# First batch of a fused attention and feed-forward kernel: the query down projection in two token halves, masks made in a room of their own, raw weights of heads 3 and 4 ahead of two stores

## The reference

```python
kv_c = kv @ W_kvc                     # 1024 -> 256
q_c = layernorm(x) @ W_dq             # 1024 -> 384
q_nope, q_rope = q_c @ W_uq, rope(q_c @ W_qr)
k_nope, v, k_rope = kv_c @ W_uk, kv_c @ W_uv, rope(kv_c @ W_kr)
scores = (q_nope . k_nope + q_rope . k_rope) / sqrt(192)
scores = where((k_ids <= seg) & (k_ids >= seg - 8), scores, -1e30)
x = x + (softmax(scores) @ v) @ W_o
```

## Time and profile before

| what | us |
|---|---|
| median of 3 runs (lowest, highest) | 3100.45 (3096.45, 3101.98) |
| the profiled execution, its own time | 3100.04 |
| its span | 3098.2 |
| PE busy | 3002.1 (97%) |
| DVE busy | 2109.3 (68%) |
| ACT busy | 1524.8 (49%) |
| POOL busy | 708.2 (23%) |

### The profile page before, as it was taken

How to read it: one execution, slowest core, us unless ns; L and a number is a source line. 1 busy time by engine, 2 the same in 40 slices (tenths; PEclk the granted TensorE clock), 3 DMA queues, 4 the chain that set the end, 5 groups by cost and what they waited for, 6 DMA issues and landing times.

```text
span 3098.2 us, 40880 instructions
## 1 busy us (share of the span) xinstructions
PE 3002.1 (97%) x14242; PEld 2432.5 (79%) x14242; DVE 2109.3 (68%) x4519; ACT 1524.8 (49%) x2983; POOL 708.2 (23%) x533
## 2 busy tenths in 40 slices
PE   7999999999999999999999999999999999999985
PEld 4788878888888878888788888888888887888862
DVE  3555657777577766777667775777757776677776
ACT  2655525555355544555345453555535554455553
POOL 6223141110411114111321114111041111411127
PEclk9999999999999999999999999999999999999985
DMA  6654456443644446344554445644364444544431
GB/s 220 228 177 165 163 212 201 146 143 117 230 157 142 142 174 218 129 144 141 183 190 144 147 137 190 208 143 136 116 237 157 146 142 174 195 135 142 146 92 4
DMA packets 163242, 496.48 MB, mean 160 GB/s; under 512 B 36689, under 2 KB 50641, under 8 KB 138337
## 3 DMA queue, kind: packets, MB, share of 16 engines
q1 hardware_dynamic: 157968, 493.00, 47.6%
q0 software_dynamic: 5072, 0.88, 0.7%
HBM read 387.68 MB, written 72.55 MB: 149 GB/s over the span
## 4 chain that ended last, share of the span: by engine, by line
PE 87%; DVE 5%; POOL 2%; DMA 2%; issue 1%; ACT 1%; SPq 0%; DVEq 0%; POOLq 0%; ACTq 0%
PE psD L2187 10%; PE psC L2196 10%; PE psE L2196 10%; PE psA L2118 8%; PE psT L2174 6%; PE psB L2127 5%; PE psA L2078 4%; PE psS L2155 4%; PE psD L2138 4%; PE psS L2161 4%; PE psS L2157 3%; PE psS L2156 3%; PE psS L2158 3%; PE psB L2078 2%; PE psA L2109 2%; PE psB L2109 2%
## 5 line engine op out<-in xcount | busy, mean ns | idle before, releaser
L1176 ACT ACTIVATE exps_ring<-exps_ring,neg_max 128x512 f32<-128x512 f32 x512 | 370.8, 724 | 421.9 <-DVE neg_max L1535 421.2
L1535 DVE CUSTOM_DVE_ANT_0 exps_ring<-psS,mask 128x512 f32<-128x512 f32 x512 | 353.1, 690 | 290.7 <-PE psS L2161 287.8
L1190 ACT ACTIVATE probsT_hi<-psT 128x512 fp32r<-128x512 f32 x472 | 282.4, 598 | 339.1 <-PE psT L2174 337.2
L1182 ACT ACTIVATE exps_ring<-exps_ring,row_sum_inverse 128x512 f32<-128x512 f32 x512 | 369.7, 722 | 60.8 <-DVE row_sum_inverse L1541 60.8
L1547 DVE TENSOR_TENSOR probsT_lo<-psT,probsT_hi 128x512 fp32r<-128x512 f32 x472 | 323.8, 686 | 55.0 <-ACT probsT_hi L1190 53.3
L2196 PE MATMUL psC<-w_o_pair,attn_hi 128*128 128x512 f32 x1016 | 333.8, 409 | 0.7 <-DVE attn_lo L1553 0.7
L2196 PE MATMUL psE<-w_o_pair,attn_hi 128*128 128x512 f32 x896 | 295.3, 410 | 0.0
L2174 PE MATMUL psT<-ident,exps_ring 128*128 128x128 f32 x1888 | 283.2, 272 | 5.6 <-DVE probsT_lo L1547 4.6
L2174 PEld LDWEIGHTS psT<-ident,exps_ring 128*128 128x128 f32 x1888 | 228.4, 140 | 76.6 <-issue 25.9
L2118 PE MATMUL psA<-q_c_hi,w_uq_ring 128*128 128x512 f32 x768 | 258.7, 391 | 2.8 <-DVE rope_term L1477 2.8
L2155 PE MATMUL psS<-k_hi,q_hi 128*128 128x512 f32 x512 | 203.5, 397 | 4.7 <-DVE q_lo L1512 2.9
(11 more groups left out here) (413 smaller groups left out, 6432.8 us busy)
## 6 DMA issues: line engine op xcount, KB each, us to landing
w_o_pair<-w_o_split SPq DMA_DIRECT2D x112, 1024.0 KB, 5.6
w_uq_ring<-w_uq_split SPq DMA_DIRECT2D x114, 384.0 KB, 3.9
w_uv_quad<-w_uv_split SPq DMA_DIRECT2D x29, 1024.0 KB, 5.0
w_uk_ring<-w_uk_split SPq DMA_DIRECT2D x114, 256.0 KB, 2.7
w_qr_sorted<-w_qr_split SPq DMA_DIRECT2D x29, 768.0 KB, 4.3
x_stage<-in_x_dram SPq DMA_DIRECT2D x32, 512.0 KB, 5.8
x_stage<-in_ctx_dram SPq DMA_DIRECT2D x32, 512.0 KB, 5.7
q_rope_stack<-rope_hi SPq DMA_DIRECT2D x256, 64.0 KB, 3.5
```

Of the source, the lines that this page charges most:

```text
L1176: act.activation(E[:, qt, :], E[:, qt, :], ACT.Exp, scale=-1.0, bias=mx[:, i % 2, qt:qt + 1], accum_out=rs[:, i % 2, qt:qt + 1]).then_inc( ...
L1182: act.activation(E[:, qt, :], E[:, qt, :], ACT.Copy, scale=ri[:, i % 2, qt:qt + 1]).then_inc(s_prob, 1)
L1535: dve.tensor_tensor_reduce(E[:, qt, :], psS[qt % 2][:, :], mask[:, qt, :], -SCALE, BIG, ALU.add, ALU.min, mx[:, i % 2, qt:qt + 1]).then_in ...
```

## The change

It touches only batch 0 (other batches run the same mask steps in the same order through new helper functions). PE turns x tiles 0 and 1, multiplies all three column blocks for tokens 0 to 255, turns tiles 2 and 3, and multiplies for tokens 256 to 511; the third block goes to psC instead of psA. ACT splits raw W_qr, W_uq and W_uk between tiles 1 and 2. SP issues raw W_qr ahead of x tile 2, and raw W_uq and W_uk ahead of x tile 3. POOL makes the masks in a room of 8 KB per partition that lies where the hi part of W_kvc is later written, so ACT waits for the masks there; the segment load comes ahead of the rstds, the first mask tile is begun ahead of the third rstd, and the others stand between the splits, all ahead of rope_lo. The wait for the splits of heads 1 and 2 moves from POOL's masks to DVE's first masked scores. The slope signs go out and back in pieces between the masks. SP loads raw W_uq and W_uk of heads 3 and 4 ahead of the two W_kvc stores. The diff, cut:

```diff
@@ rooms
             wD = sb_under("w_dq", [P, DB, QC])
+            mask_room = sb_under("first_mask_room", [P, 4, T])
@@ SP
+            raw_qr(0, qr_raw0)
             load_xs(0, 2)
-            load_xs(0, 3)
-            raw_qr(0, qr_raw0)
             for i in range(2):
                 raw_uq(0, i, uq_raw0)
                 raw_uk(0, i, uk_raw0)
+            load_xs(0, 3)
             raw_uv(0, uv_raw0)
...
             into(0, 0, 1)
-            put_kvc()
             sp.wait_ge(fullA, 4)
             sp.wait_ge(fullB, 3)
             for i in (2, 3):
                 raw_uq(0, i, uq_raw)
                 raw_uk(0, i, uk_raw)
+            put_kvc()
@@ POOL
+            load_seg(0)
+            rstds(0, [0, 1])
+            c = mask_begin(0)
+            mask_tile(c, 0, 0, lambda: rstds(0, [2, 3]))
             qr_lo(0, qr_raw0)
             for i in range(2):
                 uq_lo(0, i, uq_raw0)
                 uk_lo(0, i, uk_raw0)
+            mask_tile(c, 0, 1)
+            pool.wait_ge(s_seta, 1)
+            pool.dma_start(ss_dram, sgn64[0:NT, :]).then_inc(s_ssd, 16)
             uv_lo(0, uv_raw0)
-            masks(0, True)
+            mask_tile(c, 0, 2)
+            pool.wait_ge(s_ssd, 16)
+            pool.dma_start(ssf, ...).then_inc(s_ssb, 16)
+            mask_tile(c, 0, 3)
             rope_lo(0, 0)
+            pool.wait_ge(s_ssb, 16)
+            setup(pool.tensor_copy(ssb[:, :], ssf))
             k_rope_lo(0)
@@ ACT, prologue
+                if first:
+                    for j in range(2):
+                        stage_turned(b, j, False)
+                    qr_hi(0, qr_raw0)
+                    for i in range(2):
+                        uq_hi(0, i, 1, uq_raw0)
+                        uk_hi(0, i, 1, uk_raw0)
+                for j in range(2, TT):
                     stage_turned(b, j, False)
...
                 if first:
+                    act.wait_ge(s_mask, NM)
                     for n in range(2):
@@ DVE, mask_scores
+                if very_first and qt == 0:
+                    for slot in range(2):
+                        dve.wait_ge(s_wuq[slot], 16)
+                        dve.wait_ge(s_wuk[slot], 16)
@@ PE
+            def first_down_q(half):
+                pe.wait_ge(s_wd[0], 16)
+                pe.wait_ge(freeT, TT * (half + 1))
+                rows = slice(half * 2 * P, (half + 1) * 2 * P)
+                for col, (ps, full) in enumerate(((psA, fullA), (psB, fullB), (psC, fullA))):
+                    for c in range(DB):
+                        mm_ = pe.matmul(ps[:, rows], wD[:, c, col * P:(col + 1) * P], xT[:, c, rows],
+                                        start=c == 0, stop=c == DB - 1)
+                    if half == 1:
+                        mm_.then_inc(full, 1)
...
-            for j in range(TT):
-                turn_stage(0, j, False)
-            down_q(0)
+            for half in range(2):
+                for j in range(2 * half, 2 * half + 2):
+                    turn_stage(0, j, False)
+                first_down_q(half)
```

More of the change, by code:

```diff
@@ L182, in xattn_ffn_kernel @@
         identb = sb("ident_b", [P, P], BF16)
-        kidx = E[:, 1, :]
-        kidi = E[:, 0, :].bitcast(I32)
-        mtmp = E[:, 2:4, :]
         segi = sb("seg_int", [P, TT], I32)
@@ L839, in _, with mask_begin @@
             setup(pool.memset(nhalf[:, :], -0.5))
[L840 to L849, removed]
+            def mask_begin(b):
+                room = mask_room if b == 0 else E
+                kidi, kidx = room[:, 0, :].bitcast(I32), room[:, 1, :]
                 pool.wait_ge(s_seg, 16 * (b + 1))
@@ L855, in masks, with mask_tile, load_seg @@
                 c.do(pool.tensor_scalar(segf[:, 1, :], segf[:, 0, :], -float(LOOKBACK), None, ALU.add))
-                for t in range(TT):
[L857 to L861, removed]
+                return c
+            def mask_tile(c, b, t, between=None):
+                room = mask_room if b == 0 else E
+                kidx, lo, hi = room[:, 1, :], room[:, 2, :], room[:, 3, :]
+                c.do(pool.tensor_scalar(lo, kidx, segf[:, 1, t:t + 1], None, ALU.is_ge))
+                c.do(pool.tensor_scalar(hi, kidx, segf[:, 0, t:t + 1], None, ALU.is_le))
+                if between is not None:
+                    between()
+                c.do(pool.tensor_tensor(lo, lo, hi, ALU.mult))
+                c.do(pool.tensor_scalar(mask[:, t, :], lo, 1.0, -NEG, ALU.subtract, ALU.mult))
+            def load_seg(b):
+                pool.dma_start(segi[:, :], seg_v[b], allow_slow_non_contiguous=True).then_inc(s_seg, 16)
+            def masks(b):
+                pool.wait_ge(s_sm, b * H * TT)
+                pool.wait_ge(s_turn, b * H * TT)
+                load_seg(b)
+                c = mask_begin(b)
+                for t in range(TT):
+                    mask_tile(c, b, t)
                 assert c.n == NM
@@ L943, in _ @@
                 uk_lo(0, i, uk_raw0)
+            mask_tile(c, 0, 1)
+            pool.wait_ge(s_seta, 1)
+            pool.dma_start(ss_dram, sgn64[0:NT, :]).then_inc(s_ssd, 16)
             uv_lo(0, uv_raw0)
-            masks(0, True)
+            mask_tile(c, 0, 2)
+            pool.wait_ge(s_ssd, 16)
+            pool.dma_start(ssf, ss_dram.rearrange("(a t) j -> a (t j)", a=1).broadcast_to([P, D]))\
+                .then_inc(s_ssb, 16)
+            mask_tile(c, 0, 3)
             rope_lo(0, 0)
+            pool.wait_ge(s_ssb, 16)
+            setup(pool.tensor_copy(ssb[:, :], ssf))
             k_rope_lo(0)
@@ L994, in body @@
                     rstds(b + 1, range(2, TT))
-                    masks(b + 1, False)
+                    masks(b + 1)
                     rope_lo(b + 1, 0)
@@ L1212, in prologue @@
             def prologue(b, first):
-                for j in range(0 if first else 2, TT):
+                if first:
[6 more added lines that the diff above has]
+                for j in range(2, TT):
                     stage_turned(b, j, False)
@@ L1218, in prologue @@
                     kr_hi()
-                    qr_hi(0, qr_raw0)
-                    for i in range(2):
-                        uq_hi(0, i, 1, uq_raw0)
-                        uk_hi(0, i, 1, uk_raw0)
                     uv_hi(0, uv_raw0)
@@ L1225, in prologue @@
                 down(psB, fullB, b * BN, qc[0][:, 1, :], s_qchi)
-                down(psA, fullA, b * AN + 1, qc[0][:, 2, :], s_qchi)
+                down(psC if first else psA, fullA, b * AN + 1, qc[0][:, 2, :], s_qchi)
                 stage_turned(b, 0, True)
@@ L1670, in queries_down @@
                 qc_lo(b, 1, psB, freeB)
-                qc_lo(b, 2, psA, freeA)
+                qc_lo(b, 2, psC if b == 0 else psA, freeA)
             def prologue(b, ends=None):
@@ L2221, in down_q @@
             def down_q(b):
-                if b == 0:
-                    pe.wait_ge(s_wd[0], 16)
-                    pe.wait_ge(freeT, 2 * TT)
-                    down(psA, fullA, freeA, 0, wD, 0)
-                    down(psB, fullB, freeB, 0, wD, 1)
-                    down(psA, fullA, freeA, 1, wD, 2)
-                    return
                 pe.wait_ge(s_wdh, 16 * b)
```

8 lines of the change are left out of this document (removed).

## The result

The changed kernel takes 3087.57 us (median of 6 runs, 3084.74 to 3089.63) against 3100.27 (6 runs, 3096.45 to 3102.54): a ratio of 0.9959, with a 95% interval from 0.9949 to 0.9969, 12.7 us less. The profiled run took 3088.08, its span is 3086.3. The time is inside the forecast range, 3.6 above the forecast of 3084.0.

A forecast was written before the change was run, and what follows sets the result against it. PE, busy 97% of the span, bounds the kernel, with idle time at the start and very end. Savings of 6.0 + 2.35 + 7.8 = 16.1 us from 3100.04 gave 3083.9; range 3078 to 3091, chance 0.80.

The forecast's parts named there:

- Step 1: Query down projection in two halves on PE: starts at 14.0, ends at 39.8 instead of 45.78, saving 6.0 us.
- the bound of 2.5: Upper bound in us on low-clock loss in the projection's first block, expected at 1.7.
- Both rivals about the multiply: Down projection: weight load not hidden, 3093.5 us, chance 0.04; or fixed price per multiply, 3104 us, chance 0.03.
- Step 2: Masks made earlier on POOL, so DVE goes straight from the kvc split to the key rope: 2.35 us more.
- POOL's sum: POOL's mask tiles, splits and DMA issues after the fourth root were to add up to 54.4, when rope_lo starts.
- Step 3: Raw weights of heads 3 and 4 loaded earlier, removing ACT's wait in the first head: 7.8 us.
- Nothing, with 0.8 us to spare; bound 2 us: Cost of W_kvc stores going behind the raw loads: landed at 80.5, wanted by ACT at 81.3.
- wait in place of the one removed: Rival: stack or stores hold ACT as the load did, step 3 gives nothing, 3092 us; chance 0.09.
- an ACT wait at the first probsT_hi: Sign of being wrong: ACT waiting at its first copy of turned probabilities; no size given.
- granted clock 1.00 around 85 to 95: Sign of being right: PE at full clock from 85 to 95 us.
- a delay of 1 to 2 us costs 1 to 2: Argument against the rival of stack or stores holding ACT: a short delay costs its own length, not 7.8 us.
- The gain stays: After the prologue, order and work are the same and PE hardly waits, so the whole 16.1 us carries to the end.

The follow-up runs named there:

- the second trace: The changed kernel run once more, unchanged, beside the run with stack copies interleaved; the turn in head 2 came at 86.86 us.
- Experiments 1 and 5: 1: kernel before plus only the projection halves, 15 us slower; 5: changed kernel, x tile 3 loaded before raw weights, ratio 0.9958, and with whole projection, 3093.07 us.
- stores_first: Changed kernel with the two W_kvc stores ahead of the raw loads of heads 3 and 4; worth the same as the changed kernel within the scatter.
- one_load_then_stores: Changed kernel with the W_kvc stores right behind the first raw load, W_uq of head 3; 2.5 us faster than the changed kernel by the medians.
- whole_tiles_first: Changed kernel with the projection whole and x tiles 2 and 3 loaded ahead of the raw weights; 3093.07 us.
- stack_between_again: Repeat of the changed kernel with SP's stack copies interleaved with raw loads and stores; median 3085.40 us over 10 runs of this order.
- whole_projection: Changed kernel with the down projection whole again, 512 columns per multiply after all four turns; 5.7 us slower than the changed kernel by the medians.
- masks_in_a_row: Changed kernel with all four mask tiles made in one row after the splits; 7.8 us slower than the changed kernel by the medians.

## Why the prediction was right, by its steps

**Step 1, 6.0 us: right, measured 6.4 (5.4 in the second trace).** Start 13.92 (14.0). Blocks of 16 lie 3.45 apart, 0.2157 a multiply (0.22), half of the 0.429 of the earlier trace rows. The first block took 5.48 against 3.62 for the next, 1.9 of low clock (1.7); in other traces of this code it reached 2.9, over the bound of 2.5. The second half starts at 28.98 (29.2), and ends at 39.42 against 45.78. Tile 3's root came at 20.75, 1.4 later than before where 0.7 was expected, and nobody waited for it. Both rivals about the multiply are gone. The load is hidden: at 0.32 a multiply the blocks would lie 5.1 apart; and no fixed price: 0.429 would give 6.9. The 81 and 131 ns that the Trainium skill ("TensorE: Matmul & The Clock Gate", Back-to-back issue gap) gives for load and multiply pairs are not borne out as a ratio: these FP32 multiplies go 0.2157 and 0.429, two to one.

**Step 2, 2.35 us: right, measured 3.0.** The key rope followed the weight split at once (query 67.08, 9.32 sooner; first score 71.46, 9.35 sooner; forecast 8.35, at 72.5). Of the 1.0 beyond the forecast 0.36 is step 1, and 0.47 comes before W_kvc (48.38 against 55.21, 6.83 sooner, where the projection ends 6.36 sooner): DVE's first addition of the query rope took 1.16 before and 0.69 now, beside a mask step of POOL both times. POOL's sum missed: rope_out at 56.77, not 54.4. The later root is 0.7 of it; the rest is in one place. POOL in the changed kernel, by its timeline, at the last two mask tiles:

```profile
43.86 1.29 POOL L856 TENSOR_TENSOR first_mask_room<-first_mask_room 128x512 f32<-128x512 f32 x1
45.24 1.93 POOL L857 TENSOR_SCALAR mask<-first_mask_room 128x512 bf16<-128x512 f32 x1
...
51.46 2.35 POOL L856 TENSOR_TENSOR first_mask_room<-first_mask_room 128x512 f32<-128x512 f32 x1
53.91 2.78 POOL L857 TENSOR_SCALAR mask<-first_mask_room 128x512 bf16<-128x512 f32 x1
56.77 2.35 POOL L879 TENSOR_TENSOR rope_out<-rope_out,rope_hi 128x1024 f32<-128x1024 f32 x1
```

The same two operations took 1.9 longer while DVE subtracted w_dq_lo from 51.45 on. For PE this cost nothing (rope_out ends at 59.1, DVE's W_kvc split at 66.3), but SP's stack waits for rope_out.

**Step 3, 7.8 us: the mechanism was right, its term mis-sized: 4.9 in head 1 (6.8 in the second trace), less 0.7 of low clock in what follows the turn (none in the second).** The stall for the raw load went. What failed is the sentence "Nothing, with 0.8 us to spare; bound 2 us" on the stores. Its sum had the stack at 57.6, the stores out by 73.1 and a landing of 7.4, so 80.5. Measured: stack from 59.21 (rope_out was late by 1.6 at its end), 11.8 us long and not 10.7 (its first four copies took about 2.0 a pair, not 1.2), the store issued at 73.77 and landed in 8.5, at 82.3 (four loads at 0.5 each instead of 0.93 had given 1.6 back). Step 2 also came 1 us sooner than forecast, so ACT wanted it at 80.1 rather than 81.3. That makes a wait of 2.23, just over the bound, and here it cost more than itself: PE ran 86 to 88 at 0.50. So the "wait in place of the one removed" happened in part, and one of the forecast's own signs of being wrong, "an ACT wait at the first probsT_hi", was seen, while one of being right, "granted clock 1.00 around 85 to 95", was not. I had argued against it that "a delay of 1 to 2 us costs 1 to 2"; with the low clock behind it, it cost 2.9 in head 1 and 0.7 after it, 3.6 in all. In the second trace the wait was 1.20, the clock stayed up, and it cost 0.9: there the argument held.

**Sum:** 6.4 + 3.0 + 4.9 = 14.3, of 16.1 forecast, at the turn in head 2. Steps 1 and 2 gave 1.0 more than forecast and step 3 2.9 less, so part of the agreement is luck. "The gain stays" held only to within the scatter of the later batches: 14.5 at batch 1 and 11.9 at the end in the first trace, 16.0 and 12.3 in the second, 12.7 in the medians. The forecast said nothing of the parts' dependence on each other: it counted each step against a kernel that has the others. Experiments 1 and 5 show what this hid: the halves alone lose 15 us and gain only together with the moves of ACT's copies, the slope chain and the masks, and the early mask tile, free beside the halves, costs 1.6 us without them.

## What to carry to other kernels

When a prologue is made shorter by several us, write down every transfer that used to have slack, with its own clock (here SP's, fed by POOL), before taking the gain: the next late transfer took 3.6 of 7.8 us back in one trace and 0.9 in another. Take the landing time of a store from a row in the same crowded stretch and give it a margin (4.2 to 9.6 us for the same 1 MB here), and count how long its issue holds the queue. And try the parts of such a change alone: a step worth 6 us in its setting lost 15 without the order of work around it.

## What the runs showed of the hardware

- **An issue can hold SP several times its usual length.** SP's issue of one 1 MB store took 2.34 us at 73.77, the one 0.5 us before it 0.47, and the same store in the second trace 0.43. What held it isn't shown. The landing of W_kvc's lower part was 7.4 before, 8.5 and 8.8 in the changed kernel, 7.4 in stores_first, 9.4 in one_load_then_stores and 9.6 in whole_tiles_first; these orders differ in what is queued around it, but no run takes that apart from chance.
- **POOL and DVE sometimes slow each other.** POOL's L856 went from 1.29 to 2.35 and L857 from 1.93 to 2.78 beside DVE's two-input subtraction, DVE's scaling from 0.81 to 1.75 beside POOL's product. The Trainium skill ("SBUF — State Buffer", SBUF: two separate sides) has DVE and GpSimd share one port pair, which an instruction of GpSimd, or one of DVE with two SBUF inputs or in a 2-port mode, holds for its whole length; these rows agree, the losses being about one instruction's length or less. Another overlap doesn't show it: DVE's addition of two SBUF tiles at 46.22 in the changed kernel took its usual 0.69 us inside POOL's L857 (45.24, 1.93 us), and neither was longer.
- **Short pauses sometimes cost the clock.** After 2.29 us of idling PE ran at the 1.2 GHz level until past 88; after 1.29 (stores_first), and after 2.56 at the same place in whole_tiles_first, it did not (1.00 in all of 92 to 98). The W_kvc block behind a late context tile ran slow after pauses of 1.77 (stack_between_again, 10.11 us) and 1.88 (whole_projection, 9.24), and at full speed, 7.11, after 1.85 (masks_in_a_row). So no length of a pause decides it by itself in these rows.
